# Experts' stage of a decoder layer: TensorE's and VectorE's rounds written out in line, one register read a round on TensorE

## The reference, cut to what matters

```python
logits = x @ router_weight.T + router_bias
top_val, top_idx = jax.lax.top_k(logits, 4)
router_scores = zeros.at[tokens, top_idx].set(softmax(top_val))
gate_up = einsum('th,ehd->etd', x, gate_up_proj) + gate_up_proj_bias
gate, up = minimum(gate_up[..., ::2], 7), clip(gate_up[..., 1::2], -7, 7)
glu = gate * sigmoid(1.702 * gate)
out = einsum('etd,edh->eth', (up + 1) * glu, down_proj) + down_proj_bias
out = (out * router_scores).sum(over experts)
```

## Time and profile before

| | |
|---|---|
| median of 3 runs | 1588.98 us (1588.62 to 1595.35) |
| the profiled execution | 1591.02 us |
| its span, first to last instruction | 1589.4 us |
| TensorE busy in the span | 1454.9 us (92%) |
| VectorE, ScalarE, GpSimd busy | 962.5, 738.5, 867.6 us |
| mean granted TensorE clock | 0.960 of full speed |

### The profile page before, as it was taken

The page is one execution under the profiler, slowest core; times in us unless marked ns, Lnnn a source line. Parts: engine busy times, 40 slices in busy tenths (PEclk is TensorE's granted clock), DMA queues, the critical chain, the costliest instruction groups (busy, mean ns, idle before and its releaser), DMA issues. The chain is left out here.

```text
span 1589.4 us, 29816 instructions
## 1 busy us (share of the span) xinstructions
PE 1454.9 (92%) x7546; PEld 1027.1 (65%) x7547; DVE 962.5 (61%) x1427; ACT 738.5 (46%) x1418; POOL 867.6 (55%) x708
## 2 busy tenths in 40 slices
PE   6999999699999999988659999999999999999990
PEld 5878888444444444433548787777777777877870
DVE  2334344777878888898735555555555555555554
ACT  4212221278787788775143444444344543444233
POOL 4425333545666766745465646646566666576221
PEclk9999999899999999998669999999999999999995
DMA  6201013464576558532265546656666666473336
GB/s 213 66 21 50 13 42 56 80 97 69 92 136 128 94 113 154 95 55 69 70 219 129 151 111 155 155 124 160 133 154 153 155 170 146 117 186 75 60 57 224
DMA packets 94869, 180.64 MB, mean 114 GB/s; under 512 B 19240, under 2 KB 22056, under 8 KB 94152
## 3 DMA queue, kind: packets, MB, share of 16 engines
q1 hardware_dynamic: 75096, 133.04, 33.5%
q0 software_dynamic: 18544, 46.13, 15.6%
q10 hardware_dynamic: 1152, 0.52, 0.2%
HBM read 116.32 MB, written 33.73 MB: 94 GB/s over the span
## 5 line engine op out<-in xcount | busy, mean ns | idle before, releaser
L943 DVE TENSOR_REDUCE stage<-ps_a 128x2 f32<-128x1024 f32 x256 | 300.0, 1217 | 69.8 <-PE ps_a L1293 69.2
L2072 POOL TENSOR_TENSOR we_split<-we_raw,we_split 128x512 f32 (+1 forms) x192 | 248.5, 1535 | 103.2 <-ACT we_split L2063 103.2
L741 ACT ACTIVATE probs<-ps_b 128x512 f32<-128x512 f32 x504 | 274.2, 596 | 52.6 <-PE ps_b L1308 47.6
L2377 PE MATMUL ps_y<-we_split,hT 128*128 x912 | 233.3, 404 | 6.6 <-DVE hT L2308 3.4
L2377 PE MATMUL ps_g<-we_split,xT 128*128 x912 | 230.8, 402 | 8.4 <-issue 6.7
L2377 PE MATMUL ps_u<-we_split,xT 128*128 x912 | 231.2, 402 | 0.0
L2377 PEld LDWEIGHTS ps_g<-we_split,xT 128*128 128x128 f32 x912 | 170.6, 189 | 60.5 <-issue 21.7
L2377 PEld LDWEIGHTS ps_y<-we_split,hT 128*128 128x128 f32 x912 | 166.9, 189 | 45.0 <-issue 10.0
L2377 PEld LDWEIGHTS ps_u<-we_split,xT 128*128 128x128 f32 x912 | 166.3, 189 | 34.5
L2177 POOL DMA_INDIRECT scratch_acc<-x_keep,to_rows x76 | 121.2, 1595 | 92.9 <-issue 55.2
L2167 POOL DMA_INDIRECT x_rows<-scratch_x,from_rows x79 | 78.6, 994 | 130.8 <-ACT from_rows L2236 105.3
(11 more groups left out here) (346 smaller groups left out, 2251.0 us busy)
## 6 DMA issues: line engine op xcount, KB each, us to landing
we_raw<-in_w_expert SPq DMA_DIRECT2D x192, 256.0 KB
stack<-xT_raw SPq DMA_DIRECT2D x192, 128.0 KB, 5.4
we_bias<-in_b_expert SPq DMA_DIRECT2D x16, 768.0 KB, 4.2
stage<-in_w SPq DMA_DIRECT2D x5, 1024.0 KB, 4.8
xT_raw<-in_xT SPq DMA_DIRECT2D x4, 1024.0 KB, 6.4
x_tok<-in_x POOLq DMA_DIRECT2D x16, 256.0 KB, 3.1
acc_sb<-scratch_acc SPq DMA_DIRECT2D x8, 512.0 KB, 8.0
out<-res_sb SPq DMA_DIRECT2D x8, 512.0 KB, 4.6
```

What stands on the lines that cost most here:

```text
L741: nc.scalar.activation(probs[:, n % 3, h], src[:], ACT.Exp, scale=DH ** -0.5).then_inc(b_kept, 1)
L943: nc.vector.tensor_reduce(out[:, :, i, k % NC], ps_a[i][:], AX.X, ALU.max, negate=True).then_inc(a_kept[i], 1)
L2072: nc.gpsimd.tensor_tensor(lo, W["raw"][:, k, c], hi, ALU.subtract).then_inc(W["lo"], 1)
L2377: mm = nc.tensor.matmul(out[:], left[:, a, c], w[:, bass.ds(par, 1), k, b, c].squeeze(1), start=(n == 0), stop=(n == len(passes) - 1))
```

## The change

The helper is divided in two: how the 76 rounds are written (`rolled`, as before, or `in_line`, all 76 written out with constants), and what comes behind them, which stays. GpSimd and ScalarE keep the rolled form; VectorE and TensorE get the in-line form. On TensorE the expert's number is read once for each tile, in the middle of the `ps_u` product of the round before, and kept in a register until the tile's down product. The parity is not read but worked out as `e % 2`. The three waits on `W["hi"]` go; those on `W["lo"]` stay.

```diff
-        def loop(engine, body, end):
+        def rolled(engine, body):
             for j in range(U):
                 body(j, j)
             with engine.Fori(1, TILES // U) as r:
                 for j in range(U):
                     body(U * r + j, j)
+        def in_line(engine, body):
+            for i in range(ROUNDS):
+                body(i, i % U)
+        def rounds(engine, run, body, end):
+            run(engine, body)
             more = engine.value_load(G["active"][:, ROUNDS:ROUNDS + 1], min_val=0, max_val=1)
...
-            loop(pool, body, end)
+            rounds(pool, rolled, body, end)
-            loop(act, body, end)
+            rounds(act, rolled, body, end)
-            loop(dve, body, end)
+            rounds(dve, in_line, body, end)
...
-            def products(out, left, par, k):
+            expert = {}
+            def read_expert(i):
+                expert[i] = pe.value_load(pick(G["expert"], i), min_val=0, max_val=E_ - 1)
+            def products(out, left, par, k, ahead=None):
                 passes = [(c, a, b) for c in range(KC) for a, b in SPLITS]
                 for n, (c, a, b) in enumerate(passes):
+                    if n == len(passes) // 2 and ahead is not None:
+                        read_expert(ahead)
                     mm = nc.tensor.matmul(out[:], left[:, a, c], w[:, bass.ds(par, 1), k, b, c].squeeze(1),
...
             def down(i):
-                e = pe.value_load(pick(G["expert"], i), min_val=0, max_val=E_ - 1)
-                par = pe.value_load(pick(G["parity"], i), min_val=0, max_val=1)
-                pe.wait_ge(W["hi"], 3 * e + 3)
+                e = expert[i]
                 pe.wait_ge(W["lo"], 3 * KC * e + 3 * KC)
                 pe.wait_ge(hT_lo, i + 1)
-                if not is_at(i, 0):
+                if i > 0:
                     pe.wait_ge(y_ready, i)
-                products(ps_y, hT, par, DOWN).then_inc(y_made, 1)
+                products(ps_y, hT, e % 2, DOWN).then_inc(y_made, 1)
...
             turn_x(1, 1)
+            read_expert(0)
             def body(i, j):
-                e = pe.value_load(pick(G["expert"], i), min_val=0, max_val=E_ - 1)
-                par = pe.value_load(pick(G["parity"], i), min_val=0, max_val=1)
-                pe.wait_ge(W["hi"], 3 * e + 1)
+                e = expert[i]
                 pe.wait_ge(W["lo"], 3 * KC * e + KC)
...
-                products(ps_g, xT[:, j % 2], par, GATE).then_inc(g_made, 1)
+                products(ps_g, xT[:, j % 2], e % 2, GATE).then_inc(g_made, 1)
...
-                pe.wait_ge(W["hi"], 3 * e + 2)
                 pe.wait_ge(W["lo"], 3 * KC * e + 2 * KC)
-                products(ps_u, xT[:, j % 2], par, UP).then_inc(u_made, 1)
+                products(ps_u, xT[:, j % 2], e % 2, UP, i + 1 if i + 1 < TILES else None).then_inc(u_made, 1)
...
-            loop(pe, body, end)
+            rounds(pe, in_line, body, end)
```

## The result

The changed kernel takes **1568.37 us** (median of 4 runs, 1567.21 to 1568.62) against 1591.06 for the kernel before in runs beside it (4 runs, 1588.62 to 1595.35). The ratio is 0.986, with a 95% interval of 0.984 to 0.988: faster by 1.4%. The forecast was 1568.1 us, with a range from 1564.5 to 1577. The profiled execution took 1568.46 us, its span 1566.8.

The account below looks back on a forecast made before the run. TensorE bounds the kernel, its sequencer's table reads and branch causing pauses. Pauses -21.6, remaining wait +1.1, start -0.4 sum to -20.9 us: 1570.1 from the profiled 1591.02, less 2.04 to the median, 1568.1 us, range 1564.5 to 1577.

Parts of the forecast that it names:

- the 21.6 us to be won: TensorE in rounds 2 to 74: pauses beyond its own pace of 9.273 us a round, all 21.6 us open to be won.
- the missing branch: TensorE's sequencer ahead of `ps_g`: without the loop's branch, 0.5 us more spare time each fourth round.
- The pauses ahead of `ps_y`: 17 pauses, 6.6 us; the 14 from late gathers followed by two reads close, worth 3.2 us with refills.
- The real wait that is left: Ahead of `ps_y` in 14 rounds with ScalarE's cuts, late `hT_lo`: 0.08 us each, +1.1 us (0 to +2.1).
- `e % 2`: TensorE's 24 address calculations a round: between 0.046 and 0.098 us each, upper taken, hidden at a cost of 0.
- Rival B: TensorE's address arithmetic makes its sequencer the bound, each product 3.4 instead of 2.8 us: +137, 1705 us; chance 0.05.
- The start: Ahead of the first `ps_g` one read and one wait go, 0.75 us; taken as -0.4 us (0 to -0.75).
- The end: TensorE's 3.5 us branch behind the last round stays as far off; taken as 0, between -1.6 and +1.7 us.
- The sum: Whole kernel: -21.6 + 1.1 - 0.4 = -20.9 us, giving 1568.1 us, ratio 0.987.
- Rival A: Late GpSimd gathers replace the stalls, with pauses ahead of `ps_x` about 0.5 us each: 7 us back, 1575; chance 0.11.
- Rival C: No change: 39 code fetches each hold TensorE's sequencer 0.5 us beyond what is queued, 20 us back, 1588; chance 0.06.

Follow-up runs that it names:

- run 1: Changed kernel with TensorE's four table reads a round and its three waits on high parts back at their old places, both engines in line: 1582.2 us, ratio 0.996.
- run 2: Changed kernel with TensorE's rounds back in the hardware loop, its one read a round kept, VectorE in line: 1569.2 us, ratio 0.986.
- run 5: Changed kernel with TensorE and VectorE back in the hardware loop and the three high-part waits back, one TensorE read a round kept: 1571.4 us, ratio 0.989.
- run 3: Changed kernel with three more parity reads, values unused, in the middle of each `ps_u` product, four reads there in all: 1571.1 us, ratio 0.988.
- run 4: Changed kernel with TensorE's one read a round moved from the middle of `ps_u` to just ahead of `ps_g`: 1567.2 us, ratio 0.987.
- run 8: Changed kernel with results written by the indirect DMA without adding, so the sum over a token's experts is left out: 1563.6 us, one execution.
- run 9: The changed kernel as it is, measured again beside two others on the same chip: 1569.4 us, ratio 0.988 to the kernel before.
- run 7: Changed kernel with ScalarE's third cut behind the next round's `hT_hi` and ScalarE's rounds in line with three reads a round: 1564.7 us, ratio 0.985.
- run 11: Changed kernel with all engines in hardware loops, one TensorE read a round, no high-part waits, ScalarE's third cut behind the next `hT_hi`: 1563.5 us, ratio 0.984.
- run 6: Changed kernel with ScalarE's third cut, for the down product, moved from a round's end to behind the next round's `hT_hi`: 1562.1 us, ratio 0.982.
- run 10: Changed kernel with ScalarE's third cut later and ScalarE in line, the same kernel as an earlier run, measured again: 1562.8 us, ratio 0.983.

## Why the prediction was right

**The bound, and the 21.6 us to be won: right.** Rounds at 9.27 us in every form, and the pauses where the starts showed them. The 29 ahead of `ps_g` closed, and of the 14 behind late gathers 13; the one in round 63 came back as 0.3 us ahead of `ps_x`. Runs 1, 2 and 5 show whose doing it was: four reads in line leave 17.7 us, one read in loops with the old waits leaves 4.4. Run 3 adds that it isn't their number as such: four reads a round in the middle of `ps_u` leave 4.3. What counts is the time that the sequencer needs between its last wait and the next matmul, and so how many reads stand there: two ahead of `ps_g` were too many, one (run 4) was not. I had credited the missing branch with 0.5 us of spare time in each fourth round; that fits run 1, which took 9 us off the pauses ahead of `ps_g` (the round arithmetic went with the branch there, so the two aren't told apart), but once the reads are gone it is spare time on top of enough.

**The pauses ahead of `ps_y`: the place right, the price misread.** I took it that the two reads behind the gather's wait cost what reads cost, and called 0.97 us a length seen once. In the kernel before, 26 of the 76 reads at line 2382 took over 0.5 us. The one in round 15:

```profile
L2382 PEldq TENSOR_LOAD <-tile_expert x1: 834/834/834, 964.4 to 964.4; - x1
```

In all 14 rounds this read took 0.44 to 0.97 us in place of 0.30. Counting what it took beyond 0.30, at most the pause of its round, gives some 4.7 of their 6.4 us; this is an estimate from the 14 reads and pauses. So most of these pauses was long reads beside the scatter's packets (run 8), and the change closed them by having no read there.

**The real wait that is left: behind ScalarE's cuts, as said, but mis-sized, and for another reason.** I gave 1.1 us (0 to 2.1), as 14 rounds at 0.08. Measured: six rounds at 0.4 to 0.6 us, 3.7 in all with refills and the one in round 63. I had taken it that ScalarE's cuts keep their distance to the round before. They follow ScalarE's table reads, and in these six rounds one of the two reads ahead of the cuts took 0.6 to 0.94 us. In the kernel before, none of the reads ahead of the 14 cuts was long (0.27 to 0.29 us): the changed rhythm of the rounds put six of them beside the scatter's packets. In run 9 five were long, and five pauses were left. Run 7, with the third cut out of the way, put all of it at 0.0.

**`e % 2`: the lower bound held.** I took 0.098 us for each address; it is 46 ns, with one longer calculation a round. Nothing hung on it. Rival B is out by the same rows.

**The start: its upper end.** From the second transposes to `ps_g` pass 1.60 us, 2.32 before: 0.72 us less, of which the clock took nothing back, since `ps_u` follows `ps_g` by 5.28 us in both: the granted clock rose from 0.50 to 1.00 not at the same moment, as I had assumed, but 5.7 and 5.8 us behind the start of `ps_g`. I had said 0.4. A further 0.8 us of the 1.6 was there before the stage began, where no code differs.

**The end: missed.** I took 0 for it, between -1.6 and +1.7; it was -3.1. The branch behind the last round took 0.40 us, and `ps_h`, `ps_y` came 1.6 us sooner. The other 1.5 came from the clock, which I hadn't seen: in the kernel before the last product ran at the lower level (1.2 GHz) for 3.4 us. Its last `ps_y` took 4.6 us to VectorE's reading of it, 3.1 after the change. Over all traces the last branch took 0.37 to 0.50 us in seven, 1.96 to 3.80 in six, in the loop form and in line alike. So it isn't the form. The instruction queue tells the two groups apart: in each of the six a 16 KB packet was moving while the branch stood, and the branch ended 1.3 to 1.5 us behind that packet's end; in the seven none moved during the branch. By this timing the long branch is a wait for code. What decides whether the target is at hand, its place in the code perhaps, no run tried alone. With 1.96 us it cost nothing, with 2.4 some 0.5, with 3.0 1.0, with 3.5 and more 1.6 to 1.8 us. The lower clock in the last product came in three of the thirteen traces, one of them with a short branch (run 11); what brings it stays open.

**The sum is in part luck.** Rounds 2 to 74 gave 17.8 us, not the 20.5 of the forecast (21.6 less 1.1); the start gave 1.6, not 0.4, of which 0.8 isn't the change's; the end gave 3.1, not 0. Together that is 22.5 us, where I had 20.9. The forecast of 1568.1 us lies 0.3 from the measured median because I took it from a median of 1588.98 us for the kernel before, which in the runs beside the changed kernel was 1591.06.

**Rival A** shows once, 0.3 us in round 63; runs 3 and 6 have it at 1.0 and 1.1 us. **Rival C** is out: 32 fetches, and runs 7 and 10, with as many, have 0.0 us of pauses.

## What to carry to other kernels

Where TensorE is the bound, read the starts of its groups against the pace of undisturbed rounds; busy time and the idle column hide much of pauses of 0.1 to 0.8 us: here PE's busy time leaves 10.4 us of the window of rounds 2 to 74, and the starts show 21.6. Count what its sequencer must do between the last thing that it waits for and the next matmul: table reads at 0.65 us each were what lacked, and reading a number once and keeping it in a register did the work in a hardware loop as well as written out. Look at the longest of a sequencer's reads and not only at the median: here the long ones made most of one kind of pause. When such spare time has been made, look for which other engine's order now sets the late wait; here one moved operation on ScalarE was worth another 6 us by the medians of runs 9 to 11, of which the starts of the groups account for some 4.

## What the runs showed of the hardware

- A table read into a register took 0.27 to 0.31 us on each of the five engines (medians), and up to 1.0 us beside the packets of an indirect DMA that adds rows to memory. In the kernel before, 98% of the 56 reads over 0.5 us overlap such packets, and 13% of the short ones; of all reads that overlap them about a third was long. With a plain indirect write the longest read took 0.58 us.
- A branch on a register's value, once behind the last round, took between 0.37 and 3.80 us on TensorE in kernels whose rounds hardly differ. Where it was long (1.96 us and more) it ended 1.3 to 1.5 us behind the end of a 16 KB packet of the instruction queue; where it was short no such packet moved.
- TensorE's sequencer hid four reads a round, some 2.6 us (four times 0.64, an estimate), behind queued matmuls: run 3 has 4.3 us of pauses over 73 rounds, two profiles with one read have 3.7 and 2.7.
- Code written out for 72 rounds, one fetch of 16 KB in 19 us, cost no time that a trace shows.
